# Handing out the row maxima of a conditioned attention layer to the steps of its pipeline: counts from a model of each step's length in place of fixed counts

## The reference

```python
# layer 0: softmax attention, 16 heads of 16 channels, all pairs of 1024 tokens
xn = layer_norm(x, norm_w, norm_b)
q = (xn @ q_w + q_b).reshape(Bx, Tx, H, -1)
k = (xn @ k_w + k_b).reshape(Bx, Tx, H, -1)
att = einsum('bnhl,bmhl->bnmh', q, k) + (1.0 - mask) * -1000000.0
att = softmax(att, axis=2)
y = einsum('bnmh,bmhl->bnhl', att, v).reshape(Bx, Tx, Dx)
scale, shift = split(silu(emb) @ emb_w + emb_b)
h = layer_norm(y, sb_norm_w, sb_norm_b) * (1.0 + scale) + shift
x = x + silu(h) @ out_w + out_b
# layer 1: the same frame round a linear attention, 8 heads of 32 channels
q = softmax(q, over channels);  k = softmax(k, over tokens)
att = einsum('bnhd,bnhl->bhdl', k, v)
y = einsum('bnhd,bhdl->bnhl', q, att)
```

## Time and profile before

| | |
|---|---|
| median of 3 runs | 604.26 us (602.32 to 608.66) |
| profiled execution, its own time | 604.09 us |
| its span, first to last instruction | 602.3 us |
| granted TensorE clock, mean | 0.977 |
| busy share PE, PEld, DVE, ACT, POOL | 94%, 45%, 75%, 56%, 17% |

### The profile page before, as it was taken

One profiled execution on the slowest core, in us unless ns is written; L12 is line 12 of the kernel. 1 busy time (PEld: TensorE's weight loads), 2 busy tenths in 40 slices (PEclk: granted clock), 3 DMA queues, 4 the chain that ended last, 5 costly groups with the idle time before them and its releaser, 6 DMA issues. The chain is left out here.

```text
span 602.3 us, 8434 instructions
## 1 busy us (share of the span) xinstructions
PE 563.3 (94%) x3068; PEld 272.1 (45%) x3068; DVE 450.8 (75%) x893; ACT 337.3 (56%) x410; POOL 105.2 (17%) x175
## 2 busy tenths in 40 slices
PE   7998899999998899999989999999989999989987
PEld 6453453334333343443334444554435543525775
DVE  6687677787788998888886989769979897305644
ACT  2522565555686756468637565664765565781431
POOL 4288000340000401000020140000432001002411
PEclk9998999999999999999966999999989999999999
DMA  4273981677301122104301010011102100000002
GB/s 131 91 153 63 218 249 45 158 181 169 90 2 28 32 52 54 29 1 83 78 5 28 2 28 0 1 28 36 27 1 64 35 3 1 1 1 0 2 2 70
DMA packets 18613, 33.74 MB, mean 56 GB/s; under 512 B 3963, under 2 KB 10483, under 8 KB 17805
## 3 DMA queue, kind: packets, MB, share of 16 engines
q1 hardware_dynamic: 18462, 33.18, 22.7%
q10 hardware_dynamic: 110, 0.03, 0.0%
HBM read 19.29 MB, written 13.52 MB: 54 GB/s over the span
## 5 line engine op out<-in xcount | busy, mean ns | idle before, releaser
L895 ACT ACTIVATE prob<-sT 128x1024 f32<-128x1024 f32 x256 | 247.7, 1023 | 129.2 <-PE sT L1072 129.0
L1259 DVE TENSOR_REDUCE halfmax<-bank 128x1 f32<-128x512 f32 x424 | 269.2, 684 | 59.2 <-PE bank L957 57.1
L957 PE MATMUL bank<-ks,qs 50*128 50x512 f32 x424 | 156.3, 487 | 17.4 <-DVE halfmax L1259 11.2
L1092 PE MATMUL bank<-prob,vp 128*17 128x512 f32 x1024 | 139.0, 615 | 0.6 <-ACT prob L895 0.6
L957 PEld LDWEIGHTS bank<-ks,qs 50*128 50x128 f32 x424 | 63.8, 189 | 132.0 <-DVE halfmax L1259 76.7
L1072 PE MATMUL sT<-qs,ks 52*128 52x512 f32 x512 | 106.7, 429 | 4.9 <-DVE halfmax L1259 1.9
L667 POOL TENSOR_TENSOR rstd<-var,neghalf 128x4 f32<-128x4 f32 x12 | 12.2, 1017 | 403.2 <-DVE var L1183 403.2
L1072 PEld LDWEIGHTS sT<-qs,ks 52*128 52x128 f32 x512 | 54.6, 191 | 22.3 <-ACT prob L895 11.0
L1259 DVE TENSOR_REDUCE halfmax<-sT 128x1 f32<-128x512 f32 x88 | 56.9, 685 | 7.6 <-PE sT L957 6.5
L932 PE MATMUL bank<-w,hT 128*128 128x256 f32 x152 | 38.7, 388 | 0.3 <-ACT hT L817 0.3
L1092 PEld LDWEIGHTS bank<-prob,vp 128*17 128x17 f32 x1024 | 17.1, 96 | 40.7 <-issue 37.2
(11 more groups left out here) (182 smaller groups left out, 558.4 us busy)
## 6 DMA issues: line engine op xcount, KB each, us to landing
stack_rows<-late SPq DMA_DIRECT2D x12, 512.0 KB, 6.6
qs<-stack_rows SPq DMA_DIRECT2D x30, 192.0 KB, 3.5
ks<-stack_rows SPq DMA_DIRECT2D x14, 384.0 KB
stack_rows<-late SPq DMA_DIRECT2D x17, 256.0 KB, 5.0
xs<-in_x SPq DMA_DIRECT2D x4, 256.0 KB, 3.7
xs<-in_x SPq DMA_DIRECT2D x2, 512.0 KB, 4.6
late<-in_L_cond_emb_w SPq DMA_DIRECT2D x1, 1024.0 KB, 8.3
late<-in_L_cond_W_emb SPq DMA_DIRECT2D x1, 1024.0 KB, 11.5
```

Of the source, the lines that this page charges most:

```text
L895: act.activation(prob[:, c % 2, 2 * u:2 * u + 2, :].rearrange("p j n -> p (j n)"), sT[u][:, :], ACT.Exp).then_inc(exp_done, 1)
L957: last = pe.matmul(o, qs[rows, s % SLOTS, c, t * P:(t + 1) * P], ks[rows, hg, c, half * HALF:(half + 1) * HALF], start=True, stop=True)
L1092: last = pe.matmul(acc[32 * j:32 * j + VW, :], vp[:, b, c, hg * GH + j, :], prob[:, c % 2, 2 * u + two, :], start=(c == 0), stop=(c == NT ...
L1259: dve.tensor_reduce(halfmax[:, s % 2, r, half:half + 1], o, axis=AX.X, op=ALU.max, negate=True).then_inc(u.done, 1)
```

## The change

The counts come from a loop over the deadlines. It knows a length for each step: the sixth-power mean of TensorE's work (1.85 us, 1.95 for a product or less for other units, 0.24 or 0.13 for a piece) and VectorE's (a price for each unit, 0.69 for a piece). Whenever the pieces handed out so far fall short of what a deadline asks for, the next one goes to that step, from step 1 up to the deadline, whose length grows least by it; a step holds at most 6, and `upper` is the bound that `most` was. `places` then only says where in the step the pieces stand. The deadlines are the same, the pieces are made in the same order, and no instruction is added or taken away.

```diff
+        def has_product(k):
+            return any(key[0] not in SMALL and key[0] not in ("y", "neg") for key in pe_at[k])
+
+        def length(k, count):
+            pe_work = 1.85 + sum(PE_WORK.get(key[0], 1.95) for key in pe_at[k]) + (0.24 if has_product(k) else 0.13) * count
+            dve_work = sum(DVE_WORK[key[0]] for key in dve_mid[k] + dve_at[k]) + 0.69 * count
+            dve_work += 0.6 * sum(key[0] == "keys" and key[2] == NH - 1 for key in dve_at[k])
+            return (pe_work ** 6 + dve_work ** 6) ** (1 / 6)
...
+        for k in range(STEPS):
+            while sum(counts[:k + 1]) < min(len(stream), MAXES * ((k + 1 + LEAD) // NT + 1)) - AHEAD:
+                free = [i for i in range(1, k + 1) if counts[i] < 6 and all(sum(counts[:j + 1]) < upper(j) for j in range(i, k + 1))]
+                best = min(free, key=lambda i: length(i, counts[i] + 1) - length(i, counts[i]))
+                counts[best] += 1
...
         def places(k):
-            kinds = [key[0] for key in pe_at[k]]
-            if any(kind not in SMALL and kind not in ("y", "neg") for kind in kinds):
-                return [1, 2, 0, 2]
-            return [2, 0, 1, 0] if len(kinds) > 1 else [2, 1, 0, 0]
...
+            if k == 0:
+                return [0, 2, 1, 2]
+            if has_product(k):
+                return ([0, 0, 0, 0], [1, 0, 0, 0], [1, 1, 0, 0], [1, 2, 0, 0], [1, 1, 0, 2], [1, 2, 0, 2], [2, 2, 0, 2])[counts[k]]
+            return ([0, 0, 0, 0], [1, 0, 0, 0], [2, 0, 0, 0], [2, 1, 0, 0] if len(pe_at[k]) < 2 else [2, 0, 1, 0], [2, 1, 1, 0], [3, 1, 1, 0], [3, 1, 2, 0])[counts[k]]
...
-            count = places(k) if k > 0 else [0, 2, 1, 2]
-            most = min(len(stream), MAXES * (s + 2 + int(c >= 3))) - taken_to
-            least = max(min(len(stream), MAXES * ((k + f + 1 + LEAD) // NT + 1)) - taken_to - sum(most_of[k + 1:k + f + 1]) for f in range(min(2 * NT, STEPS - k)))
-            total = max(min(sum(count), most), min(least, most_of[k]))
```

More of the change, by code:

```diff
@@ L315, in two_layer_conditioned_attention @@
                 dve_at[begins["T", kind, b, h, KC - 1] + 1].append(("silu", kind, b, h))
-        def places(k):
-            kinds = [key[0] for key in pe_at[k]]
-            if any(kind not in SMALL and kind not in ("y", "neg") for kind in kinds):
-                return [1, 2, 0, 2]
-            return [2, 0, 1, 0] if len(kinds) > 1 else [2, 1, 0, 0]
-        LEAD = 2
-        most_of = [6] * NT + [5] * (STEPS - NT)
+        PE_WORK = {"T": 0.5, "kT": 0.5, "qT": 0.5, "y": 0.45, "neg": 0.3, "vec2": 0.3, "embT": 0.5, "att": 1.0, "y1": 1.0}
@@ new lines, in two_layer_conditioned_attention @@
+        DVE_WORK = {"stats": 0.38, "aggr": 0.75, "silu": 1.1, "y": 0.75, "neg": 0.3, "qk": 0.75, "out0": 0.7, "out1": 0.7, "keys": 0.75,
+                    "queries": 1.4, "qsum": 1.2, "recips": 0.7, "y1": 0.7, "att": 0.35, "vec2": 0.2, "embT": 0.5, "cond": 0.2}
+        LEAD = 2
+        def has_product(k):
[5 more added lines that the diff above has]
+            return (pe_work ** 6 + dve_work ** 6) ** (1 / 6)
@@ new lines, in two_layer_conditioned_attention, with upper @@
+        counts = [0] * STEPS
+        counts[0] = 5
+        def upper(k):
+            return min(len(stream), MAXES * (k // NT + 2 + int(k % NT >= 3))) - AHEAD
+        for k in range(STEPS):
[3 more added lines that the diff above has]
+                counts[best] += 1
@@ L330, in two_layer_conditioned_attention @@
+        def places(k):
+            if k == 0:
[3 more added lines that the diff above has]
+            return ([0, 0, 0, 0], [1, 0, 0, 0], [2, 0, 0, 0], [2, 1, 0, 0] if len(pe_at[k]) < 2 else [2, 0, 1, 0], [2, 1, 1, 0], [3, 1, 1, 0], [3, 1, 2, 0])[counts[k]]
         runs, taken_to = [], AHEAD
         for k in range(STEPS):
-            s, c = divmod(k, NT)
@@ L333, in two_layer_conditioned_attention @@
-            count = places(k) if k > 0 else [0, 2, 1, 2]
-            most = min(len(stream), MAXES * (s + 2 + int(c >= 3))) - taken_to
-            least = max(min(len(stream), MAXES * ((k + f + 1 + LEAD) // NT + 1)) - taken_to - sum(most_of[k + 1:k + f + 1]) for f in range(min(2 * NT, STEPS - k)))
-            total = max(min(sum(count), most), min(least, most_of[k]))
-            for place_of in (3, 2, 1, 0):
-                while sum(count) > total and count[place_of] > 0:
-                    count[place_of] -= 1
@@ L340, in two_layer_conditioned_attention @@
-            for place_of, limit in ((0, 3), (2, 3), (1, 3)):
-                while sum(count) < total and count[place_of] < limit:
-                    count[place_of] += 1
+            count = places(k)
             ends = [taken_to + sum(count[:i + 1]) for i in range(4)]
```

## The result

Over 13 executions each, the changed kernel has a median of 598.56 us (595.30 to 603.44), the kernel before 608.66 us (601.27 to 614.23); its first three, shown above, had 604.26. The ratio is 0.9929, 95% interval 0.9901 to 0.9958. It leaves out executions over 1.5% above the fastest of the same kernel, six of the 13 of the kernel before, so it shows less than the medians do (0.983). The time is inside the predicted range, but the forecast of 17.8 us less was too much by far: 4 us by the ratio, 4.1 between the two profiled executions (599.97 for 604.09), 10 by the medians.

A forecast was written before the change was run, and what follows sets the result against it. TensorE and VectorE were taken to bound the kernel in turn, with clock falls as a third thing. Stretch terms summed to -17.8 us (clock 8.0, schedule 9.8), so 604.1 would become 586.3 us, range 579 to 599.

The forecast's parts named there:

- the clock: Steps 66 to 71 and 98 to 104: granted clock counted as regained, 6.7 and 1.3 us, 8.0 in all.
- rival 1: Whole kernel: the schedule gains but an equally long clock fall comes elsewhere, 593.0 us; chance 0.17.
- rival 4: Steps 20 to 33 and 53 to 65: steps of four starve TensorE, keeping its clock at 1.2 GHz, 609 us; chance 0.04.
- what leaves the fives: Plain steps with five pieces: each piece taken off gives back 0.53 to 0.59 us.
- the fourths: Plain steps raised from three pieces to four: 0.40 us each taken, between bounds 0.07 and 0.53.
- The sixth in a product step: Product steps raised from five pieces to six: 0.12 us each taken, ends -0.1 and 0.35.
- Step 36 with four: 2.6: Step 36 with four pieces would take 2.6 us, within 16.7 for steps 34 to 39.
- the 4.6 forecast: Steps 34 and 35, pieces falling from ten to three, would take 4.6 us together.
- Steps 42 to 46: Steps 42 and 43 -1.2 us with three pieces less, 44 -0.8, 46 +0.4.
- rival 2: Added pieces cost their upper ends, 28 fourths at 0.53 and 20 sixths at 0.35: 594.5 us; chance 0.12.
- the idle time of the pieces' weight loads behind reductions: Sign in the changed profile: TensorE's weight loads for the maxima idle well under 76.7 us waiting for VectorE.
- Rival 3: Banks had already evened the steps out, moves cancel and the clock falls once again: 603 us; chance 0.09.

The follow-up runs named there:

- the first experiment: Kernel before with each matmul of a maximum in steps 34, 35, 66, 67, 100 and 101 done twice: 597.46 us against 604.34, ratio 0.9925.
- experiment 5: Maxima left out: 18 sixths of the changed kernel, 589.91 us; second, 28 fourths of the changed kernel, 587.19; third, 24 of the fives, kernel before, 583.68.
- experiments 4, 8 and 3: 3: changed kernel with at most five pieces in a product step, the sixths moved to other steps, 598.69 us, ratio 0.9940; experiment 4 and experiment 8 have their own lines.
- experiment 7: Kernel before's counts, changed kernel's `places`, pieces moved from twelve fives to plain or transposing steps of three: 24 moved 588.84 us, 12 moved 589.75; changed kernel again 597.52.
- experiment 8: Kernel before's counts with 17 pieces moved from the same twelve plain steps to product steps, five to six there: 596.10 us, about 592 at full clock.
- experiment 4: Changed kernel, same counts, the sixth piece of a product step put behind the values matmuls instead of ahead of the scores: 598.59 us, ratio 0.9932.
- experiment 6: Changed kernel with each maximum's reduction reading 256 of its 512 columns: 573.01 us, at full clock 572.9 and 573.1.
- the control: Kernel before with the maxima's matmuls done twice in steps 44, 60, 61, 76, 85 and 90 instead: 608.25 us against 602.57, ratio 1.0078.

## Why the prediction was right and wrong

Its terms against the measured ones, at full clock: the kernel before from the first experiment, the changed kernel from its second profile, both without a fall in the steps but one in step 83. The first has the doubled matmuls in it.

| steps | forecast | measured |
|---|---|---|
| 1 to 19 | +0.6 | -1.0 |
| 20 to 33 | +3.6 | +3.6 |
| 34 to 39 | -3.7 | -2.9 |
| 40 to 52 | -1.2 | **+2.3** |
| 53 to 65 | +1.7 | +1.6 |
| 66 to 71, clock apart | -3.7 | -2.9 |
| 72 to 84 | -2.0 | **+2.4**, 1.6 of it the clock in steps 83 and 84 (13.9 us; 12.3 in the second kernel of experiment 5, at 1.00) |
| 85 to 90 | +1.3 | +2.4 |
| 91 to 97 | -3.1 | -3.2 |
| 98 to 104, clock apart | -3.1 | -3.3 |
| 105 to 117 | -0.2 | **+1.8** |
| schedule | -9.8 | -0.8, with the 1.6 taken off |

**Right: the clock.** That it would come back, and why (TensorE idle behind five reductions and four statistics). The forecast counted 8.0 us; most executions of the changed kernel still have a short fall, as the 0.994 of most of them shows, so some 3 us of that are not there. Part of these falls is rival 1 in small: both profiles have one in step 83, behind 2.66 of 3.50 us of busy TensorE. Other orders have theirs in steps 45, 80 and 98 (experiments 4, 8 and 3), where the kernel before has none; the one with 24 moves and no new sixth has none at all. The rule of the Trainium skill ("TensorE: Matmul & The Clock Gate", "A second HAM failure mode: psum-queue depth-cycling") names TensorE's short idle times between groups of matmuls as what makes the clock go to and fro. The trace agrees for the two worst steps of the old order (busy 2.51 and 2.19 of 3.50 us, then 1.2 GHz); the feared fall in the many steps with four pieces (rival 4) never came, they ran at 1.00 in both profiles of the changed kernel.

**Right: what leaves the fives gives 0.53 to 0.59** (0.60 measured, experiment 5), and the fourths cost about the 0.40 that was taken (0.33 in the 24 places of experiment 7, 0.47 in the 28 of the change).

**Wrong: the step "The sixth in a product step: ... Ends -0.1 and 0.35, taken 0.12, as most such steps leave VectorE spare time."** In the change a sixth costs 0.53 (experiment 5), in the kernel of experiment 8 it costs 0.40 by the whole and 0.51 by the steps' own lengths, all above the upper end of 0.35. Twenty of them at 0.4 over the forecast are 8 us of the 9 that the schedule missed, and the three stretches in bold are those with 13 of the 20. The rest is several errors that nearly cancel: the steps emptied (below), 1.1 us in 85 to 90, and against them 1.6 us that steps 1 to 19 did better than forecast although they hold six sixths, mostly because step 2 fell from 6.02 to 4.57 us when step 1 took two pieces more. The pair it was read from was unlike: steps 4 and 5 follow a transposing step of four pieces and take over little, steps 18 and 19 follow product steps and take over the eviction of a `qk`. Step 19, with its own neighbours, goes from 5.00 to 5.28. And VectorE's idle share was no spare time: in steps 40 to 52 VectorE was busy 47.49 of 56.02 us, and one piece more, with five sixths, cost 2.3 us.

**Wrong in size: the steps emptied to one or two.** They give 0.8 us less than forecast in 34 to 39 and in 66 to 71. The failed term is "Step 36 with four: 2.6": it took 3.86, the joining in it (experiment 5); 34 and 35 took 4.19 for the 4.6 forecast. Steps 42 to 46, of which the forecast asked 1.6 us, gave 0.15 with three pieces less, in the kernel before and in the changed one:

```profile
219.32:235.22 15.90, 14.85 (x90) 6.08 (x89) 14.49 (x35) 11.22 (x13) 3.40 (x6) 1.00 0.00 1
```

```profile
221.94:237.69 15.75, 14.54 (x88) 5.84 (x87) 13.43 (x32) 11.09 (x12) 3.40 (x6) 1.00 0.00 0
```

The change spends its dear sixths to buy these.

**The rivals.** The outcome is rival 2, its mechanism (the added pieces cost more than taken), but carried by the sixths, beyond its own upper end of 0.35, plus a little of rival 1 in the short falls. Of the signs named for the forecast, the idle time of the pieces' weight loads behind reductions went the other way: 87.4 us, where "well under 76.7" was asked. Rival 3's arithmetic (nothing from the schedule) came true, by a bad trade between cheap and dear places; how much soft borders between steps add (steps 9 and 10, 42 to 46) isn't separated.

**Open.** What a sixth's half microsecond is made of. A second place in the step is no cheaper (experiment 4), and VectorE's rate is only part of all waits (experiment 6, 22.5 us in 477 pieces). Not separated: TensorE's own time for it against the round of the three banks.

## What to carry to other kernels

Split a time by its granted clock before crediting a schedule: two orders of the same work may differ only in how often the clock fell. Where a planner weighs two engines, measure the price of the next unit in each kind of step by leaving it out or moving it, with the same neighbours; idle time in a busy share is not capacity. Look where the units that hang on the last one (here the joining) come to stand, too. Prices that are nearly equal (0.47, 0.53, 0.60) tell that most moves trade nothing: move only from the dearest to the cheapest kind, and stop there.

## What the runs showed of the hardware that I had not expected

Thirty matmuls that only write once more what is there cost at most some 2 us at full clock and won 7 by the medians, because they stood where TensorE waited: behind 3.15 of 3.5 us of busy TensorE in step 66 the clock stayed at 2.4 GHz, behind 2.51 (2.49 in the control) it fell to 1.2. The fall is a matter of chance for one execution: behind 2.50 of 3.5 us in step 34 nothing fell, and the kernel before was granted between 0.955 and 1.00 in its executions beside the experiments (but for one of 831.75 us, at 0.554), and its time followed, from 614.9 to 595.3 us.
